# First loads of a cross-attention and feed-forward kernel: x issued by ScalarE instead of SyncE

## What is computed

```python
x = x + _L0_xattn_ref(_layernorm(x), ctx, Wq, bq, Wk, bk)     # one head, attends over 128 tokens
x = x + _L0_ffn_ref(_layernorm(x), W, b, A, B, gate_w, gate_b)  # dense layer and a routed low-rank part
x = x + _L1_xattn_ref(_layernorm(x), ctx, mask, ...)          # 32 query heads, 8 key and value heads
x = x + _L1_ffn_ref(_layernorm(x), gate, up, down)            # gated, 4-bit weights with scales and zeros
```

```python
Q = jnp.einsum('btx,dx->btd', text, Wq) + bq
K = jnp.einsum('bpx,dx->bpd', features, Wk) + bk
scores = jnp.einsum('btd,bpd->btp', Q, K) * scale
attended = jnp.einsum('btp,bpd->btd', softmax(scores), features)
```

## Time and profile before

| | us |
|---|---|
| median of 3 runs | 818.98 (818.36 to 820.65) |
| profiled execution, its own time | 818.81 |
| its span, first to last instruction | 817.0 |
| TensorE busy | 804.4 (98%) |
| VectorE busy | 570.9 (70%) |
| ScalarE busy | 544.0 (67%) |
| GpSimd busy | 533.8 (65%) |
| bytes moved, whole kernel | 131.77 MB, mean 161 GB/s |

### The profile page before, as it was taken

How to read it: one execution, slowest core, us unless ns; L and a number is a source line. 1 busy time by engine, 2 the same in 40 slices (tenths; PEclk the granted TensorE clock), 3 DMA queues, 4 the chain that set the end, 5 groups by cost and what they waited for, 6 DMA issues and landing times.

```text
span 817.0 us, 13206 instructions
## 1 busy us (share of the span) xinstructions
PE 804.4 (98%) x3914; PEld 668.7 (82%) x3914; DVE 570.9 (70%) x1022; ACT 544.0 (67%) x1781; POOL 533.8 (65%) x537
## 2 busy tenths in 40 slices
PE   9999999999999999999999999999999999999996
PEld 7887888888788888888888888888887868888884
DVE  6977746334666666666666666666667999999997
ACT  5453732346777777777777777777767578888883
POOL 1453822432777777777777777777755337999998
PEclk9999999999999999999999999999999999999999
DMA  8414767615676666666667676666645055566322
GB/s 317 151 52 117 180 163 225 128 39 151 196 196 193 194 189 181 188 188 186 187 185 226 189 223 200 179 188 191 181 142 206 1 117 135 141 150 156 77 39 104
DMA packets 96455, 131.77 MB, mean 161 GB/s; under 512 B 25760, under 2 KB 68896, under 8 KB 96352
## 3 DMA queue, kind: packets, MB, share of 16 engines
q1 hardware_dynamic: 93936, 119.13, 49.2%
q0 software_dynamic: 2016, 11.01, 7.2%
q10 hardware_dynamic: 432, 0.79, 0.3%
HBM read 91.74 MB, written 42.29 MB: 164 GB/s over the span
## 4 chain that ended last, share of the span: by engine, by line
PE 89%; POOL 3%; DMA 2%; DVE 2%; ACT 2%; issue 1%; SPq 1%; POOLq 0%; DVEq 0%; ACTq 0%
PE pair L1798 20%; PE pair L1800 20%; PE pair L1799 19%; PE pair L2008 8%; PE pair L2009 8%; PE pair L2102 6%; PE pair L1847 3%; PE pair L1821 1%; DMA land<-block_bounce 1%; DMA resid<-in_x_dram 1%; PE pair L1899 1%; PE pair L1955 1%; POOL kv L798 1%; PE pair L1932 1%; DMA block_bounce<-tb 1%
## 5 line engine op out<-in xcount | busy, mean ns | idle before, releaser
L1798 PE MATMUL pair<-split,xnT_hi 128*128 128x512 f32 x288 | 112.6, 391 | 0.3 <-issue 0.3
L1800 PE MATMUL pair<-split,xnT_lo 128*128 128x512 f32 x288 | 112.1, 389 | 0.0
L1799 PE MATMUL pair<-split,xnT_hi 128*128 128x512 f32 x288 | 112.1, 389 | 0.0
L1081 ACT ACTIVATE headT<-land,wqk 128x512 f32<-128x512 f32 x62 | 44.9, 724 | 88.3 <-DMA land<-block_bounce 63.7
L1798 PE MATMUL pair<-split,aoT_hi 128*128 128x512 f32 x244 | 95.8, 392 | 0.0
L1800 PE MATMUL pair<-split,aoT_lo 128*128 128x512 f32 x244 | 95.2, 390 | 0.0
L1799 PE MATMUL pair<-split,aoT_hi 128*128 128x512 f32 x244 | 94.9, 389 | 0.0
L1092 ACT ACTIVATE prob<-pair,nmax 128x128 f32<-128x128 f32 x244 | 86.0, 363 | 11.9 <-DVE nmax L1576 11.2
L821 POOL TENSOR_TENSOR prob<-prob,rinv 128x512 f32<-128x512 f32 x61 | 63.6, 1042 | 43.1 <-DVE rinv L1547 43.1
L1666 DVE SCALAR_TENSOR_TENSOR kv<-pair,gu_s,kv 128x1024 f32<-128x1024 f32 x65 | 83.3, 1282 | 9.7 <-PE pair L2009 5.0
L2008 PE MATMUL pair<-xnT_hi,split 128*128 128x512 f32 x224 | 88.1, 393 | 1.3 <-DVE kv L1719 1.0
(11 more groups left out here) (231 smaller groups left out, 2117.1 us busy)
## 6 DMA issues: line engine op xcount, KB each, us to landing
block_bounce<-tb SPq DMA_DIRECT2D x244, 128.0 KB, 2.3
land<-block_bounce SPq DMA_DIRECT2D x61, 512.0 KB, 3.3
raw<-in_wqo_dram SPq DMA_DIRECT2D x62, 256.0 KB, 3.0
kv<-in_ffn_w_dram SPq DMA_DIRECT2D x12, 768.0 KB, 4.3
kv<-negated_zeros POOLq DMA_DIRECT2D x12, 768.0 KB, 6.3
kv<-key_bounce SPq DMA_DIRECT2D x32, 128.0 KB, 2.9
key_bounce<-tb SPq DMA_DIRECT2D x44, 64.0 KB, 2.2
kv<-in_ctxT_dram SPq DMA_DIRECT2D x2, 1024.0 KB, 11.8
```

Of the source, the lines that this page charges most:

```text
L1798: pe.matmul(dst, l_hi, r_hi, start=first, stop=False)
L1799: pe.matmul(dst, l_hi, r_lo, start=False, stop=False)
L1800: return pe.matmul(dst, l_lo, r_hi, start=False, stop=last)
```

## The change

ScalarE, not SyncE, issues the three transfers of x. On ScalarE they stand between the high parts of chunks 1 and 2. SyncE's order is then chunks 0 and 1, the bias, chunks 2 to 7, the transposed context, and the rest as before. Nothing else is changed: the same transfers with the same semaphores, and the same order of all other work on every engine.

```diff
@@ SyncE
-            def load_rows(g):
-                tiles = slice(*X_GROUPS[g])
-                sp.dma_start(resid[:, tiles, :], x[tiles].rearrange("b p d -> p b d")).then_inc(s_x[g], 16)
-
             for e in range(KT):
                 load(2 * e, wk0[e])
                 load(2 * e + 1, wq0[e])
                 if e == 0:
                     sp.dma_start(bias[:], bqk).then_inc(s_bq, 16)
-                if e == 2:
-                    load_rows(0)
-                    load_rows(1)
-            load_rows(2)
             for h in range(2):
@@ ScalarE
-            for c in range(FIRST):
+            for c in range(2):
+                hi(c)
+            for g, tiles in enumerate(X_GROUPS):
+                rows = slice(*tiles)
+                act.dma_start(resid[:, rows, :], x[rows].rearrange("b p d -> p b d")).then_inc(s_x[g], 16)
+            for c in range(2, FIRST):
                 hi(c)
```

## The result

| | before | after |
|---|---|---|
| median of 17 runs | 819.0 us | 822.67 us |
| span of the profiled execution | 817.0 us | 819.5 us |

The ratio is 1.0042, with a 95% interval of [1.0034, 1.0049]: by the ratio the change costs 3.4 us (3.7 by the medians) where 1.3 were forecast, and the time lies above the range. (One run of each kernel, over 2900 us, was disturbed, and the ratio leaves it out.) The sign was right, the size was not.

The account below looks back on a forecast made before the run. TensorE was taken as the bound nearly everywhere, with x1's landing on the path in the first 20 us. +1.25 us by x1 and +0.05 for VectorE gave +1.3 us, a median of 820.3 us; range 818.4 to 822.2.

Parts of the forecast that it names:

- x1: Second transfer of x (tiles 2 and 3), on the path at the start; forecast to land at 12.9 instead of 11.65 us.
- The issue at 4.15: ScalarE's issue of x0, the first transfer of x, forecast at about 4.15 us, at dispatch of its second high part.
- the half share: ScalarE's queue was taken to get half the transfer engines beside SyncE's, so x0 and x1 need 2.10 MB more moved.
- the lag of 0.46 MB: At the kernel's start, a transfer counts as landed some 0.46 MB after its place in the order of transfers.
- a third's share: Same case as Rival 3: x gets a third of the engines.
- a block of ScalarE: Rival 4: x's issues block ScalarE and the high part of chunk 2 starts late; 821.5 us, chance 0.06.
- Rival 3: x gets a third of the engines at the start; x1 at 15.5, +3.9 us, 822.9 us; chance 0.08.
- the start of ScalarE's queue: x's first bytes move 1.2 us after the issue, at 5.35 us, when 1.03 MB have moved.
- the prediction's own second way: Descriptors served in order of issue: all eight weight chunks lie ahead of x1, 2.10 + 1.05 + 0.46 = 3.61 MB.

Follow-up runs that it names:

- two queues without the context beside them: The changed kernel, with SyncE waiting for the landing of x1 before it issues the transposed context: 820.03 us, ratio 1.0018 to the kernel before.
- two queues in the old order: The changed kernel, but ScalarE issues only x's first two transfers; SyncE issues chunks 6 and 7 after chunk 2 lands, then x's third: 819.14 us, 1.0002.
- only the place: The kernel before, with all three transfers of x still on SyncE but behind chunks 6 and 7: 819.52 us, ratio 1.0013.
- the change, 9 products: The changed kernel with 9 unread products of ones added where TensorE waits for low parts of chunks 6 and 7: 821.23 us, ratio 1.0041.
- the change once more: The changed kernel run again unaltered, against the kernel before: 822.6 us, ratio 1.005.
- the change, same chip: The changed kernel unaltered, run on the same chip as the one with 9 added products: 822.68 us, ratio 1.0054 to the kernel before.
- x behind chunk 2's part: The changed kernel, but ScalarE issues x behind the high part of chunk 2 rather than chunk 1: 825.33 us, ratio 1.0082.

## Why the prediction was wrong

**What held.** x1 is on the path and its lateness passes through one for one: +2.44 us at x1, +2.43 at TensorE's stretch, +2.5 on the span. The issue at 4.15 (4.18), the half share (q10 56.0%, q1 48.0%), and the lag of 0.46 MB held too, and neither a third's share nor a block of ScalarE that mattered was seen. Rival 3 was priced at 822.9, next to what was measured, but for x1 at 15.5 by a share of a third; that its time is near is chance. Statistics, the last low parts and the transposes moved as described.

**The step that failed first: the start of ScalarE's queue.** The prediction took 1.2 us from issue to first byte, from ScalarE's stores at the end of the kernel. It is 3.0 us here, 3.2 and 3.4 us in the two other traces of the change, and 2.05, 2.4 and 3.6 us in the experiments with the other issue times and the order kept. These rows were read as a delay, though they fit a place as well: at 810.98 SyncE had issued two stores (0.52 MB), and by 812.25 (147 GB/s for a microsecond, 383 for the next, 0.10 MB after) 0.63 MB had moved, so ScalarE's first bytes came when those ahead were through. At 4.18 SyncE had issued six chunks and was issuing the seventh, with which they are 1.84 MB, and x started after 1.52 MB, not 1.03. That is 0.49 MB or 1.2 us, which takes the forecast of +1.25 to the measured +2.44.

The prediction had this very thought: served in the order of issue, x1 would stand behind all eight chunks. It set it beside the half share as another way to the same 3.6 MB, and so as a confirmation. The two aren't alternatives, they add up: first x waits for its place, then its rate is halved by the context behind. The runs took them apart: the place alone costs 1.1 us (x on SyncE's queue behind the chunks), two queues without the context beside them 1.5 us, two queues in the old order nothing that the times show (0.9 us of x1 in the trace). On the share, the Trainium skill (DMA: Bandwidth & Descriptors, section "Queues, rings and completion order") says that each engine goes round between the queues that have work; the trace of the change from 8 to 14 us agrees (q10 56.0%, q1 48.0%).

**The cost that wasn't seen: TensorE's clock.** The prediction followed TensorE's wait only as a delay. In the change it grows to about 2 us or more, and in some executions TensorE comes out of it at half its clock: 0.57 and 0.59 from 17 to 21 us behind waits of 2.16 and 2.62 us, 1.00 behind 1.96, 1.36 and 1.00 us. Two of the three traces of the change have it. With the wait half filled it is gone. What it costs can be read in the time from x1 to the stretch of 64 products, which starts at 45.30 in the kernel before:

```profile
45.30 7.14 PE pair L1899 x64
```

| trace | x1 | stretch of 64 | between | granted clock, 17 to 21 us |
|---|---|---|---|---|
| before | 11.65 | 45.30 | 33.65 | 1.00 |
| two queues, old order | 12.53 | 46.16 | 33.63 | 1.00 |
| only the place | 13.07 | 46.68 | 33.61 | 1.00 |
| the change | 14.09 | 47.74 | 33.65 | 1.00 |
| the change, 9 products | 14.56 | 48.15 | 33.59 | 1.00 |
| the change once more | 14.53 | 49.10 | 34.57 | 0.57 |
| the change, same chip | 15.10 | 49.58 | 34.48 | 0.59 |
| x behind chunk 2's part | 17.69 | 52.17 | 34.48 | 0.50 (21 to 23 us) |

With the clock at 1.00 the way takes 33.6 us for every x1 from 11.65 to 14.56, with the fall 0.8 to 0.9 us more. The timed runs have it too: of the 26 undisturbed runs of the change, the five with a mean granted clock of 1.0 over the whole kernel took 820.6 to 821.4 us, the ten with 0.996 or 0.997 took 821.7 to 823.6, and of 51 runs of the kernel before none is under 0.998. So the 3.4 us of the timed runs are the late start and the share, an x1 that landed still later in the two other traces, and in many runs the clock.

**The range** ended at 822.2 since it took the issue-to-byte time as certain and put the clock at nothing. A start bounded from both sides, 1.2 us by the earlier trace rows and "all issued bytes first" by the prediction's own second way, would have given 1.84 + 2.10 + 0.46 = 4.40 MB, about 14.9 us and +3.2, which is 822.2 for the median. The measured 822.67 needs some of the clock's 0.9 us on top of it.

**Open.** What sets the start when large transfers are just ahead: behind 4.2 MB of issued bytes x started after 2.32, behind 1.84 after 1.52, behind 1.57 (order kept) after 1.31. That it is the bytes ahead, and not the work of issuing them, is argued and not shown: no run changed the one without the other. Also why x1 lands at 14.09, 14.53 and 15.10 in three executions of the same kernel, and where some of the lateness goes: in the trace on the same chip the stretch of 64 is 4.28 us late and the span only 3.1, with two queues in the old order 0.86 and 0.1.

## What to carry to other kernels

A transfer that was moved to another engine's queue did not overtake the chunks issued well before it here, and from there on it shared the engines with everything that the first queue went on to issue: keep what is needed first ahead in time of issue, and hold back what is needed last. Where two ways of reckoning give the same number, ask whether they exclude each other or add up. When a wait of TensorE grows past what the trace of before has, price the clock behind it too.

## What was not expected of the hardware

Two queues shared evenly only once both were under way; the first packet of the second came 1.27 to 3.6 us after its issue, and at the kernel's start the later the more had been issued ahead (2.05, 2.4, 3.0 to 3.4 and 3.6 us behind 0.26, 1.57, 1.84 and 4.2 MB). Three issues by ScalarE took 1.57 to 3.08 us for the same transfers in different executions. Added work of 2 us on TensorE made the changed kernel 1.4 us faster, 0.9 of it by the clock that it held.
